# Last expert pair, mixes, result and output of a fused perceiver layer in two column halves

## The reference

```
x   = layernorm(x);  se = layernorm(slot_embeds) * scale
logits   = einsum('bnd,esd->bnes', x, se)
dispatch = softmax(logits, axis=1)
combine  = softmax(logits.reshape(b, n, 16 * 64), axis=-1)
slots = einsum('bnd,bnes->besd', x, dispatch)
gate  = gelu(einsum('besd,edf->besf', slots, Wg) + bg)      # f: 512
up    = einsum('besd,edf->besf', slots, Wu) + bu
eout  = einsum('besf,efo->beso', gate * up, Wd) + bd        # o: 256
out   = x_in + einsum('bns,bso->bno', combine, eout.reshape(b, 1024, 256))
```

## Time and profile before

| | |
|---|---|
| median of 3 runs (lowest, highest) | 194.73 us (194.56, 194.84) |
| the profiled execution | 193.85 us |
| its span, first to last instruction | 191.8 us |
| TensorE (PE) busy | 185.5 us, 97% |
| its weight loads (PEld) | 143.3 us, 75% |
| VectorE (DVE) / ScalarE (ACT) / GpSimd (POOL) | 65% / 57% / 43% |
| granted TensorE clock | 1.000 of full speed |
| chain that ended last | PE 93%, ACT 3%, DMA 2%, DVE 1% |

### The profile page before, as it was taken

How to read it: one execution, slowest core, us unless ns; L and a number is a source line. 1 busy time by engine, 2 the same in 40 slices (tenths; PEclk the granted TensorE clock), 3 DMA queues, 4 the chain that set the end, 5 groups by cost and what they waited for, 6 DMA issues and landing times.

```text
span 191.8 us, 3900 instructions
## 1 busy us (share of the span) xinstructions
PE 185.5 (97%) x1236; PEld 143.3 (75%) x1236; DVE 125.0 (65%) x269; ACT 109.2 (57%) x226; POOL 82.4 (43%) x61
## 2 busy tenths in 40 slices
PE   6999999999999999999999999999999999999993
PEld 4888999999999999999899989873544544444351
DVE  3567988787777778778877788743673522534331
ACT  3568687677677767768767344958268321122210
POOL 2777978788777678877677021100000000000000
PEclk9999999999999999999999999999999999999999
DMA  5999958848784875984592499999999999974200
GB/s 182 315 368 377 327 167 276 266 126 230 244 278 150 278 242 125 349 240 135 157 244 64 121 394 386 350 378 363 387 359 382 256 379 270 284 188 97 46 0 27
DMA packets 24907, 47.01 MB, mean 245 GB/s; under 512 B 1600, under 2 KB 11968, under 8 KB 24896
## 3 DMA queue, kind: packets, MB, share of 16 engines
q1 hardware_dynamic: 23664, 43.52, 69.7%
q10 hardware_dynamic: 1232, 3.35, 7.4%
HBM read 46.73 MB, written 0.13 MB: 244 GB/s over the span
## 4 chain that ended last, share of the span: by engine, by line
PE 93%; ACT 3%; DMA 2%; DVE 1%; issue 0%; SPq 0%; ACTq 0%
PE bank L658 15%; PE bank L409 11%; PE bank L672 7%; PE bank L450 6%; PE bank L454 6%; PE bank L452 6%; PE bank L422 6%; PE bank L426 6%; PE bank L424 6%; PE bank L435 6%; PE bank L682 2%; PE bank L545 2%; PE bank L689 2%; DMA W_sb<-in_L_xattn_W_dram 2%; PE bank L564 2%; ACT seT L841 1%
## 5 line engine op out<-in xcount | busy, mean ns | idle before, releaser
L953 POOL TENSOR_TENSOR c_lo<-raw,c_hi 128x1024 fp32r<-128x1024 f32 (+1 forms) x25 | 54.0, 2161 | 20.2 <-ACT c_hi L753 20.1
L1031 DVE TENSOR_TENSOR cT_lo<-bank,cT_hi 128x512 fp32r<-128x512 f32 (+1 forms) x50 | 31.8, 675 | 10.6 <-ACT cT_hi L780 9.3
L780 ACT ACTIVATE cT_hi<-bank 128x512 fp32r<-128x512 f32 (+1 forms) x48 | 25.7, 585 | 10.1 <-PE bank L409 10.1
L450 PE MATMUL bank<-c_hi,pT_hi 128*128 128x258 f32 x98 | 29.9, 305 | 0.0
L454 PE MATMUL bank<-c_hi,pT_lo 128*128 128x258 f32 x98 | 27.7, 282 | 0.0
L452 PE MATMUL bank<-c_lo,pT_hi 128*128 128x256 f32 x98 | 27.5, 281 | 0.0
L948 POOL TENSOR_TENSOR c_hi<-raw,zero 128x512 fp32r<-128x512 f32 (+1 forms) x25 | 25.7, 1027 | 1.4 <-DMA raw<-in_ctx_dram 1.4
L409 PE MATMUL bank<-tab,raw 128*128 128x128 f32 x196 | 25.8, 273 | 0.2 <-DVE cT_lo L1031 0.2
L787 ACT ACTIVATE pT_hi<-bank 128x512 fp32r<-128x512 f32 (+1 forms) x25 | 14.8, 590 | 14.1 <-PE bank L435 14.0
L409 PEld LDWEIGHTS bank<-tab,raw 128*128 128x128 f32 x196 | 22.1, 141 | 1.0 <-issue 0.3
L422 PE MATMUL bank<-cT_hi,q_hi 128*128 128x512 f32 (+1 forms) x50 | 21.5, 430 | 0.0
(11 more groups left out here) (171 smaller groups left out, 293.9 us busy)
## 6 DMA issues: line engine op xcount, KB each, us to landing
raw<-in_ctx_dram SPq DMA_DIRECT2D x24, 512.0 KB, 4.0
bias<-biases_dram ACTq DMA_DIRECT2D x10, 320.0 KB, 7.4
late_gu<-in_L_ffn_Wg_dram SPq DMA_DIRECT2D x3, 1024.0 KB, 10.8
late_gu<-in_L_ffn_Wu_dram SPq DMA_DIRECT2D x3, 1024.0 KB, 11.2
late_d<-in_L_ffn_Wd_dram SPq DMA_DIRECT2D x3, 1024.0 KB, 13.6
early_gu<-in_L_ffn_Wg_dram SPq DMA_DIRECT2D x4, 512.0 KB, 5.1
early_gu<-in_L_ffn_Wu_dram SPq DMA_DIRECT2D x4, 512.0 KB, 4.8
early_d<-in_L_ffn_Wd_dram SPq DMA_DIRECT2D x4, 512.0 KB, 5.0
```

What stands on the lines that cost most here:

```text
L450: nc.tensor.matmul(bank[6 + r][:, 0:D + 2], ph, c_hi[:, slot, t, :], start=(t == 0), stop=False)
L780: nc.scalar.activation(cT_hi[:, g % 2, h, 0:n], bank[h][:, 0:n], ACT.Copy).then_inc(cThi_rdy, 1)
L953: nc.gpsimd.tensor_tensor(c_lo[:, slot, 0:nt, :], raw[:, slot, 0:nt, :], c_hi[:, slot, 0:nt, 0:D].bitcast(fp32), ALU.subtract).then_inc(cl ...
L1031: nc.vector.tensor_tensor(cT_lo[:, g % 2, h, 0:n], bank[h][:, 0:n], cT_hi[:, g % 2, h, 0:n].bitcast(fp32), ALU.subtract).then_inc(cTlo_rdy, 1)
```

## The change

Four things are changed. **Mixes**: every mix is two matmuls of 128 columns, one for each half of the 256 output columns, into banks 1 and 5; mix 0 now waits for both halves of `combT`, since bank 5 was used by its transposes. **Last transposes**: the transposes of pair 7 go two by two to banks 3 and 0; ScalarE copies the first two (256 columns), VectorE the other two, under a semaphore of its own, `hidT2_rdy`. **Last down projection** (`last_down`): first all chunks for output columns 0 to 127 into bank 4, then for 128 to 255 into bank 6, with a bias add for each half. **Last mix, result, output**: by the same halves; the output is sent in two transfers of 64 KB whose rows are 512 bytes long.

```diff
@@ -350,9 +353,10 @@
             for p in range(WSLOTS, PAIRS):
                 reload_hidden(p)
                 reload_down(p)
-            sp.wait_ge(res_rdy, 1)
-            sp.dma_start(out[0, :, :], x1[:, :]).then_inc(st_out, 16)
-            sp.wait_ge(st_out, 16)
+            for h in range(2):
+                sp.wait_ge(res_rdy, h + 1)
+                sp.dma_start(out[0, :, cols(h)], x1[:, cols(h)]).then_inc(st_out, 16)
+            sp.wait_ge(st_out, 32)
 
 
         LT_BANK = (6, 7, 1)
@@ -362,9 +366,9 @@
         UP_BANK = (2, 0)
         SE_BANK = (6, 4, 2, 6)
         V_BANK, FREQ_BANK, CONV_BANK = (2, 0), (4, 1), (5, 3)
-
-        def cols(h):
-            return slice(h * P, (h + 1) * P)
+        MIX_BANK = (1, 5)
+
+        LAST_T_BANK, LAST_DOWN_BANK = (3, 0), (4, 6)
 
 
         @block.tensor
@@ -674,6 +678,34 @@
                                                 start=(c == 0), stop=(c == FC - 1))
                 last.then_inc(down_ps, 1)
 
+            def last_down():
+                p = PAIRS - 1
+                s = p % WSLOTS
+                pe.wait_ge(ld_wd[s], 16)
+                pe.wait_ge(eout_rdy, p)
+                for h in range(2):
+                    for c in range(FC):
+                        if c < 2:
+                            pe.wait_ge(hidT_rdy, p + 1)
+                        else:
+                            pe.wait_ge(hidT2_rdy, 1)
+                        for a in range(2):
+                            last = nc.tensor.matmul(bank[LAST_DOWN_BANK[h]][a * SL:(a + 1) * SL, 0:P],
+                                                    hidT[:, c, a * SL:(a + 1) * SL],
+                                                    w_d(s, a, a + 1)[:, 0, c, cols(h)],
+                                                    start=(c == 0), stop=(c == FC - 1))
+                    last.then_inc(down_ps, 1)
+
+            def last_transpose():
+                p = PAIRS - 1
+                pe.wait_ge(hid_rdy, p + 1)
+                pe.wait_ge(hidT_rdy, p)
+                for half in range(2):
+                    for c in (2 * half, 2 * half + 1):
+                        last = nc.tensor.transpose(bank[LAST_T_BANK[half]][:, (c % 2) * P:(c % 2 + 1) * P],
+                                                   hid[:, c * P:(c + 1) * P], ident)
+                    last.then_inc(hidT_ps, 1)
+
             def hidden_transpose(p):
                 pe.wait_ge(hid_rdy, p + 1)
                 if p >= 1:
@@ -684,11 +716,15 @@
 
             def mix_of(p):
                 pe.wait_ge(eout_rdy, p + 1)
-                if p in (0, 4):
-                    pe.wait_ge(combT_rdy, p // 4 + 1)
-                last = nc.tensor.matmul(bank[1][:, 0:D], combT[:, p, :], eout[:, p % 2, :],
-                                        start=(p == 0), stop=(p == PAIRS - 1))
-                last.then_inc(mix_ps, 1)
+                if p == 0:
+                    pe.wait_ge(combT_rdy, 2)
+                for h in range(2):
+                    if p == PAIRS - 1:
+                        pe.wait_ge(eout_rdy, p + 1 + h)
+                    last = nc.tensor.matmul(bank[MIX_BANK[h]][:, 0:P], combT[:, p, :], eout[:, p % 2, cols(h)],
+                                            start=(p == 0), stop=(p == PAIRS - 1))
+                    if h == 1 or p == PAIRS - 1:
+                        last.then_inc(mix_ps, 1)
 
             for p in range(PAIRS + 1):
                 if p < PAIRS:
@@ -705,7 +741,9 @@
 
                 if p == PAIRS:
                     mix_of(PAIRS - 3)
-                if p >= 2:
+                if p == PAIRS:
+                    last_transpose()
+                elif p >= 2:
                     hidden_transpose(p - 1)
                 if p == 3:
                     mix_of(0)
@@ -722,7 +760,9 @@
                 if p == 2:
                     transpose_dispatch(2)
                     combine_transpose(0)
-                if p >= 1:
+                if p == PAIRS:
+                    last_down()
+                elif p >= 1:
                     down_of(p - 1)
                 if p == 2:
                     gather(2)
@@ -919,8 +959,13 @@
                 act.wait_ge(hidT_ps, p + 1)
                 if p >= 1:
                     act.wait_ge(down_ps, p)
-                nc.scalar.activation(hidT[:, :, :].rearrange("p c s -> p (c s)"), bank[3][:, :], ACT.Copy
-                                     ).then_inc(hidT_rdy, 1)
+                if p == PAIRS - 1:
+
+                    nc.scalar.activation(hidT[:, 0:2, :].rearrange("p c s -> p (c s)"),
+                                         bank[LAST_T_BANK[0]][:, 0:2 * P], ACT.Copy).then_inc(hidT_rdy, 1)
+                else:
+                    nc.scalar.activation(hidT[:, :, :].rearrange("p c s -> p (c s)"), bank[3][:, :], ACT.Copy
+                                         ).then_inc(hidT_rdy, 1)
                 if p >= 1 and p - 1 + BSLOTS < PAIRS:
 
                     act.wait_ge(eout_rdy, p)
@@ -1248,7 +1293,17 @@
                     dve.wait_ge(cexp_rdy, 2)
                     link(nc.vector.tensor_tensor(rs[:, 2:3], rs[:, 0:1], rs[:, 1:2], ALU.add))
                     link(nc.vector.reciprocal(rs[:, 3:4], rs[:, 2:3]))
-                if p >= 1:
+                if p == PAIRS:
+                    dve.wait_ge(hidT_ps, p + 1)
+                    nc.vector.tensor_copy(hidT[:, 2:4, :].rearrange("p c s -> p (c s)"),
+                                          bank[LAST_T_BANK[1]][:, 0:2 * P]).then_inc(hidT2_rdy, 1)
+                    dve.wait_ge(mix_ps, p - 2)
+                    for h in range(2):
+                        dve.wait_ge(down_ps, p + h)
+                        nc.vector.tensor_tensor(eout[:, (p - 1) % 2, cols(h)], bank[LAST_DOWN_BANK[h]][:, 0:P],
+                                                bias[:, (p - 1) % BSLOTS, 2 * F + h * P:2 * F + (h + 1) * P], ALU.add
+                                                ).then_inc(eout_rdy, 1)
+                elif p >= 1:
                     dve.wait_ge(down_ps, p)
                     if p >= 3:
                         dve.wait_ge(mix_ps, p - 2)
@@ -1258,9 +1313,10 @@
                 if p == 2:
                     copy_slots(2)
 
-            dve.wait_ge(mix_ps, PAIRS)
-            nc.vector.scalar_tensor_tensor(out=x1[:, :], in0=bank[1][:, 0:D], scalar=rs[:, 3:4], in1=x2[:, :],
-                                           op0=ALU.mult, op1=ALU.add).then_inc(res_rdy, 1)
+            for h in range(2):
+                dve.wait_ge(mix_ps, PAIRS + h)
+                nc.vector.scalar_tensor_tensor(out=x1[:, cols(h)], in0=bank[MIX_BANK[h]][:, 0:P], scalar=rs[:, 3:4],
+                                               in1=x2[:, cols(h)], op0=ALU.mult, op1=ALU.add).then_inc(res_rdy, 1)
 
 
 def spectrum_tables(np, n):
```

More of the change, by code:

```diff
@@ L185, in perceiver_kernel @@
         gs_rdy = sem("gs_rdy")
-        shift_rdy = sem("shift_rdy")
+        shift_rdy, hidT2_rdy = sem("shift_rdy"), sem("hidT2_rdy")
         spec_ps, spec_rdy = sem("spec_ps"), sem("spec_rdy")
@@ L272, in transpose_xh, with cols @@
                                         ).then_inc(xhT_ps, 1)
+        def cols(h):
+            return slice(h * P, (h + 1) * P)
         block = st.enter_context(nc.Block())
```

## The result

| | before | after |
|---|---|---|
| executions side by side | 22 | 22 |
| median (lowest, highest) | 194.69 us (193.83, 196.51) | 193.60 us (192.88, 195.18) |
| profiled execution, its span | 193.85, 191.8 us | 192.96, 190.9 us |
| ratio after / before | | 0.9937 (95%: 0.9916 to 0.9959) |

The change makes the kernel faster, by less than 1%: 0.9937 of 194.73 us is 193.50 us, 1.23 less, with an interval from 0.80 to 1.64 less. The two profiled executions differ by only 0.89. The ratio is that of the means, 193.62 and 194.85 us, and so not quite that of the medians. The ratios leave out executions more than 1.5% above the fastest of their kernel, none in this table and 5 of the 35 of before in the next one. The prediction was -0.78 and 193.95, in a range from 193.55.

The account below looks back on a forecast made before the run. The prediction took TensorE, busy 97% of the span, and from 185.26 us one dependent thread of engines to bound the kernel. Terms summed to -0.78 us, taking the median from 194.73 to 193.95, range 193.55 to 194.95.

Parts of the forecast that it names:

- 1. earlier mixes: Mixes of pairs 0 to 6: two 128-column matmuls replacing one of 256 cost +0.04 us in all.
- 2. start of the projection: Last down projection: split copies let it start at 185.60 instead of 185.91, -0.31 us, with PE itself late next.
- 3. projection by halves: Last down projection: 32 records of 128 columns replacing 16 of 256 cost +0.03 us, time going with columns.
- 5. output: End of kernel: two 64 KB transfers, the second issued 0.47 us after the first, gain 0.07 us.
- Steps 2 to 4: Last pair: projection start -0.31 us, projection by halves +0.03, then halved add -0.13, mix -0.21, result -0.13.
- rival A: Last projection: small records do not shrink with their columns, 0.112 us each, +1.85 us, total 195.77; chance 0.08.
- B: Last projection: load and matmul overlap only in part, 0.158 us a pair, +0.80 us, total 194.72; chance 0.07.
- Rival C: Output: second transfer queues behind the first, costing up to 1.1 us more, total up to 195.12; chance 0.09.
- Rival D: Tail: only half the shortening, because a seemingly free engine is not, -0.3 us, total 194.4; chance 0.06.
- How the numbers follow: Whole kernel: forecast 193.95 us at chance 0.70, own range 193.6 to 194.3; faster 0.73, slower 0.10, same 0.17.
- The profiled execution: Whole kernel: profiled run 193.85 us, median 194.73, 0.88 higher; the same difference was applied to the changed kernel.

Follow-up runs that it names:

- the ladder: Partial versions of the change against before: split mixes and result 0.9962, early projection start added 0.9987, halved tail without early start 0.9978; full change again 0.9936.
- mixes: Kernel before with only the mixes and the result by halves; one projection, add and output transfer: 194.40 us, ratio to before 0.9962.
- e2_one_output: Kernel after with one output transfer of 128 KB instead of two: 194.07 us in its one execution.
- paced: Before and after, each with 16 extra TensorE work groups ahead of real work: 207.47 and 206.82 us; with bias loads also issued earlier, medians 0.84 apart.
- the first two comparisons: Kernel after, unedited, against before in two sessions: 193.60 us, ratio 0.9937, then 193.52 us, ratio 0.9936.
- the third: Kernel after with ScalarE issuing the next bias loads before its wait for the transposes, against before: 193.53 us, ratio 0.9957.
- tail: Kernel after with the last transposes in one bank and one 512-column ScalarE copy, as in before: 194.65 us, ratio to before 0.9978.

## Why the prediction was right in its terms and wrong in its range

Term by term, from the distances of after and before and from the ladder:

| step | predicted | measured | from |
|---|---|---|---|
| 1. earlier mixes | +0.04 | +0.08 | `mixes`, 31.35 - 31.27 |
| 2. start of the projection | -0.31 | -0.31 | 31.04 - 31.35 |
| 3. projection by halves | +0.03 | +0.02 | 1.97 against 1.95 |
| 4. add | -0.13 | -0.13 | 0.29 against 0.42 |
| 4. mix | -0.21 | -0.21 | 188.01 to 188.53, against 188.39 to 189.12 |
| 4. result | -0.13 | -0.13 | 0.35 against 0.48 |
| 5. output | -0.07 | -0.15 | `e2_one_output`, and 1.97 against 2.12 |
| sum | -0.78 | -0.83 | -0.86 by the distances; -0.89 by the profiled executions; -0.84 paced |

**Steps 2 to 4 held.** PE itself was what came late next: ACT's copy was done at 185.48 and PE was free at 185.65, so the chunks waited for PE, not it for them. This is why leaving out VectorE's copy cost nothing. From the first mix of before (154.64) the projection starts at 185.68, 0.08 behind the predicted 185.60; that is what the seven mixes cost, twice the 0.04 put down for them in step 1.

**Step 3 decided the sign.** The 32 records ran in pairs, 0.109 us per pair or 0.055 each, with no room for rival A (0.112) or B (a pair at 0.158). The rule of the Trainium skill, "TensorE: Matmul & The Clock Gate", section "Back-to-back issue gap", 81 ns a matmul of 128 columns, does not hold here: by it the stretch would have taken an estimated 2.6 us, and it took 1.97. These are 64-wide weights that run two at a time in two column groups, and the measurement decides.

**Step 5 was mis-sized,** at less than half. The step took a value between bounds of -0.17 and +1.1 for which no row stood. The term lies almost at its lower bound, so the first transfer costs the second little: 0.02 by that bound. With it the sum would have been -0.86. Rival C was wrong: two transfers of one array in a row at the end did not behave like the two loads of the start. Rival D was wrong too, SP's second issue standing 0.47 behind the first, as written.

**What failed is the range,** in the step "How the numbers follow", and ahead of it the step "The profiled execution". The forecast's own range took the spread of the three executions shown (194.56 to 194.84) for the uncertainty of the measurement. Those three stood close together by chance. 22 executions of the same kernel reach from 193.83 to 196.51, by the two draws above, and its median in the sessions was 194.69, 195.26, 195.96 and 194.49. The profiled execution at 193.85, 0.88 under the median, was the warning in the prediction itself: it applied the same difference to the kernel after and did not ask what the 0.88 was. It was an execution in which the clock had risen before the first matmul on W. For after the difference is 0.64 (192.96 against 193.60). Of the 0.35 us by which the median came out under 193.95, 0.11 are the sum of the terms (step 5 above all) and 0.24 this carried-over difference. So the change itself is worth 0.83 to 0.86 us on the path, and 0.84 between the paced kernels, whose spread is 0.1 us before and small for most of after. The timed -1.23, with an interval from -0.80 to -1.64, just contains that, and the forecast's 0.9960 (193.95 / 194.73) lies just outside. The lowest executions stand 0.95 and 0.91 us apart in the first two comparisons and 0.68 in the third (with the earlier biases). That the rest of the 1.23 is a fall of the draws in favour of after fits all this, but it is argued and not shown: the first two comparisons gave 0.9937 and 0.9936, and both draws are larger than what is to be explained.

Two things stay open: the high executions of the paced kernels after, and whether the change also makes a slow start or a late bias rarer. Its code has no edit at either, it even issues the biases of pair 5 0.04 us later after the first mix (13.34 against 13.30), and no run here shows it.

## What to carry to other kernels

At the end of a kernel, where each engine only hands on to the next, cut the last tile in halves: each link then shows only its second half, and the links gained 0.13, 0.21, 0.13 and 0.15 us while the matmuls in halves cost 0.02. When a prediction rests on a profiled execution, ask what separates it from the median before giving a range; when effects of under 1% are to be told apart, measure distances inside the trace, or make the varying stretch the same in every execution. A partial version of an edit must keep the number and order of its waits, or the joints (0.06 us each here) hide what it was to show. Where a page gives the clock as full speed, look at the durations too: the trace may hold no record of it there.

## What the runs showed of the hardware

- Two 64-wide float32 matmuls of 128 columns side by side in the array step by 0.109 us together, 0.055 each; a 128-wide one takes 0.11. Loads of 137 ns each (32 in 1.73 us) hide in it.
- The start of the kernel runs at half rate for a while that differs from one execution to the next, up to 2.1 us in all, though the page's clock row shows no lower digit there: full speed is on record only from 4.08 to 9.27 us on, and nothing ahead of it. The durations have to be read: the same four records in 0.97 or 1.88 us.
- Waits in another number or order than before became an instruction of their own ahead of the work they hold back. In `tail` it is this (duration min/median/max in ns, first and last start):

```profile
L688 PEldq EVENT_SEMAPHORE  x1: 51/51/51, 187.4 to 187.4; - x1
```

It starts when the copy is done (187.33), and the first load comes 0.11 us after the copy instead of 0.05.
- A transfer of 64 KB, issued 0.47 us behind another, brings the end 0.15 us nearer to its issue than one of 128 KB.
